# When GpSimd splits the operands of a causal attention round: two orders of one queue

## The reference

```python
x = x + 0.5 * ffn(ln(x))            # receptance and key mix with the token before
x = x + causal_attention(ln(x))     # 16 heads of 8 channels
x = x + 0.5 * ffn(ln(x))            # the same weights again
x = x + 0.5 * mixture(ln(x))        # 8 experts, the best 2 of each token
x = x + focus_attention(ln(x))      # up to 3 iterations of a second attention
x = x + 0.5 * mixture(ln(x))
```

```python
xr = mu_r * x + (1 - mu_r) * x_prev
xk = mu_k * x + (1 - mu_k) * x_prev
out = sigmoid(xr @ W_r.T) * (square(relu(xk @ W_k.T)) @ W_v.T)        # ffn

a = where(causal, q @ k.T * HD ** -0.5, -inf)                         # attention
a = clip(a, -100, 100); e = exp(a - max(a))
p = e / (sum(e) + 1e-6) + 1e-8
o = (p / sum(p)) @ v; out = o @ w_proj.T
```

## Time and profile before

| | |
|---|---|
| median of 3 runs | 1373.71 us (1372.26 to 1373.77) |
| the profiled execution's own time | 1369.53 us |
| its span, first to last instruction | 1367.8 us |
| mean granted TensorE clock | 0.966 of full speed |
| TensorE busy (share of the span) | 1217.5 us (89%) |
| VectorE busy | 920.0 us (67%) |
| ScalarE busy | 842.2 us (62%) |
| GpSimd busy | 533.9 us (39%) |
| first 50 us | setup |
| 50 to 382 us | the 16 causal rounds |
| 382 us to the end | mixture, focus attention, mixture |

### The profile page before, as it was taken

The page is one execution under the profiler, slowest core; times in us unless marked ns, Lnnn a source line. Parts: engine busy times, 40 slices in busy tenths (PEclk is TensorE's granted clock), DMA queues, the critical chain, the costliest instruction groups (busy, mean ns, idle before and its releaser), DMA issues. The chain is left out here.

```text
span 1367.8 us, 36731 instructions
## 1 busy us (share of the span) xinstructions
PE 1217.5 (89%) x12275; PEld 781.6 (57%) x12275; DVE 920.0 (67%) x2874; ACT 842.2 (62%) x1549; POOL 533.9 (39%) x817
## 2 busy tenths in 40 slices
PE   4689899898759999999889988999899997999998
PEld 3456566566537777777544433444344443767876
DVE  3578888887746874677677745666766665677444
ACT  3467777776433344443677877899787885333543
POOL 6366766766430040401344433344333331032344
PEclk9799999999959999999999999999999999999999
DMA  6323323324204022111545544445434441001332
GB/s 162 93 66 93 97 58 104 92 64 106 53 7 139 3 76 84 55 32 52 142 120 155 151 126 113 144 137 141 126 111 126 122 119 39 1 28 41 102 115 85
DMA packets 113582, 125.77 MB, mean 92 GB/s; under 512 B 14988, under 2 KB 90020, under 8 KB 113450
## 3 DMA queue, kind: packets, MB, share of 16 engines
q1 hardware_dynamic: 110378, 117.82, 30.6%
q0 software_dynamic: 3072, 6.30, 1.5%
HBM read 79.89 MB, written 44.05 MB: 91 GB/s over the span
## 5 line engine op out<-in xcount | busy, mean ns | idle before, releaser
L1469 ACT ACTIVATE e_buf<-ps_q 128x1024 f32<-128x1024 f32 x192 | 196.9, 1026 | 58.0 <-PE ps_q L2194 57.7
L2207 PE MATMUL ps_o<-e_buf,v_st 128*32 128x256 f32 x3072 | 210.7, 393 | 5.1 <-POOL v_st L1081 4.2
L1469 ACT ACTIVATE e_buf<-ps_k 128x1024 f32<-128x1024 f32 x192 | 197.0, 1026 | 7.5 <-PE ps_k L2194 7.4
L2054 PEld LDWEIGHTS ps_o<-w,e_buf 128*128 128x128 f32 x1280 | 152.2, 193 | 13.1 <-issue 12.0
L2054 PE MATMUL ps_o<-w,e_buf 128*128 128x128 f32 x1280 | 158.4, 277 | 0.0
L2622 DVE TENSOR_REDUCE mx<-ps_q 128x10 f32<-128x640 f32 x128 | 104.9, 820 | 45.0 <-PE ps_q L1752 44.1
L1290 ACT ACTIVATE e_buf<-ps_k 128x768 f32<-128x768 f32 x128 | 103.0, 805 | 46.2 <-PE ps_k L1764 45.3
L2207 PEld LDWEIGHTS ps_o<-e_buf,v_st 128*32 128x32 f32 x3072 | 81.5, 110 | 76.6 <-issue 40.3
L940 POOL TENSOR_SCALAR_AFFINE_SELECT e_buf<-e_buf 128x512 f32<-128x512 f32 x128 | 85.6, 669 | 89.8 <-ACT e_buf L1290 86.9
L1385 ACT ACTIVATE e_buf<-ps_q,b_t 128x512 f32<-128x512 f32 x80 | 54.6, 685 | 90.5 <-PE ps_q L2046 86.7
L1385 ACT ACTIVATE e_buf<-ps_k,b_t 128x512 f32<-128x512 f32 x80 | 54.0, 685 | 71.0 <-PE ps_k L2046 67.6
(11 more groups left out here) (392 smaller groups left out, 2746.5 us busy)
## 6 DMA issues: line engine op xcount, KB each, us to landing
k_st<-scr_x SPq DMA_DIRECT2D x128, 256.0 KB
q_st<-scr_q SPq DMA_DIRECT2D x256, 96.0 KB
scr_q<-parts SPq DMA_DIRECT2D x64, 192.0 KB, 2.0
scr_x<-parts SPq DMA_DIRECT2D x48, 192.0 KB, 2.0
q_st<-scr_q SPq DMA_DIRECT2D x128, 64.0 KB
slots_in<-heads_out SPq DMA_DIRECT2D x3, 1536.0 KB
slots_out<-heads_out SPq DMA_DIRECT2D x18, 256.0 KB
heads_out<-slots_in SPq DMA_DIRECT2D x15, 256.0 KB
```

Of the source, the lines that this page charges most:

```text
L1469: act.activation(e_buf[g % 2][:, hp * 2 % HG:hp * 2 % HG + 2, :], (ps_q, ps_k)[hp % 2][:, :, :], ACT.Exp).then_inc(sem("fast_exp"), 1)
L2054: last = mm(ps_o[:, e % 2, t * P:(t + 1) * P], h_sb[e % 2][:, f, t * P:(t + 1) * P], w2[:, e * NF + f, :], start=f == 0, stop=f == NF - 1)
L2207: last = mm(ps_o[at:at + VW, p, low:low + T], v_st[p][:, kt, h, :], e_buf[g % 2][:, j, kt * T:(kt + 1) * T], start=g == 0 and kt == 0, sto ...
```

## The change

Only GpSimd's program of a causal round is changed; no instruction is added to the kernel and none taken away. L916 and L920, which split the operands of a sequence, move from round n (for sequence n + 1, between masks 2 and 3) to the end of the round before, between mask 8 and the addition of the second ffn. L924 moves from behind mask 3 to the place between the mix step and mask 2. The square and the sum of the first ffn now follow mask 3 directly.

```diff
             def causal_round(n, p, half):
                 first, second, after = within(n, 0, B - 4), within(n, 2, B), within(n, 0, B - 2)
-                parts_next = within(n, 1, B - 2)
                 causal_keep(n, 0)
                 if first:
                     mix_step(mix1(n + 3), norm1(n + 3))
+                if within(n, 1, B - 2):
+                    causal_last_parts(n + 1)
                 causal_keep(n, 1)
-                if parts_next:
-                    causal_parts(n + 1)
                 causal_keep(n, 2)
-                if parts_next:
-                    causal_last_parts(n + 1)
                 if first:
                     mix_square(mix1(n + 3))
                     mix_gate(mix1(n + 3))
...
                 causal_keep(n, 7)
+                if within(n, 0, B - 3):
+                    causal_parts(n + 2)
                 if second:
                     mix_add(mix2(n - 2), n - 2)
```

## The result

The changed kernel is slower. Its median is 1382.21 us (5 runs, 1378.81 to 1385.82), before's 1373.71 us (5 runs, 1372.26 to 1374.62); the ratio is 1.0069, 95% interval 1.0045 to 1.0093. The profiled execution took 1382.21 us with a span of 1380.4 us, against 1369.53 and 1367.8.

A forecast was written before the change was run, and what follows sets the result against it. No engine is full; a cycle through the engines bounds the kernel, with VectorE not idling in its longest stretch. Rounds 2 to 12 at +0.86 us plus edges give +9.2 us, forecast 1382.9 us, range 1371 to 1391.

The forecast's parts named there:

- (b): VectorE's idle gap behind L2668, waiting for TensorE's row scores: 0.36 us a round, forecast to become 0.
- Step 1: At the round's end L916 holds up VectorE's pair L2576, so the row maxima come 0.54 us later.
- Step 2: TensorE's next row scores and VectorE's second row maxima both move by the same 0.54 us.
- Step 4: L924 blocks VectorE's L2592, then mask 2 blocks L2593, which ends 1.65 us later.
- Step 5: From L2593 to L2668 order and length stay; the square no longer makes TensorE wait.
- (a): VectorE's stretch without idling from the last row maxima to L2668's end: 12.31 us, forecast 13.96.
- Step 6: Behind the second row maxima wait, L2593 no longer meets mask 5: 2.89 us becomes 2.46; the round is +0.86 us.
- (c): VectorE's stretch from the end of its idle gap to the end of the two L2576: 2.89 us, forecast 2.46.
- (d): Stretch in which TensorE works from the transposes to the last row scores: 5.11 us, forecast unchanged.
- The number of rounds and the edges: Rounds 2 to 12 at +0.86 us each, round 1 +0.4, rounds 13 and 14 -0.36 each; +9.2 us in all.
- the gain comes through: Rival: VectorE gets the port whenever it asks, 12 rounds lose at least 0.36 us, 1369.4 us; chance 0.17.
- half the price: Rival: VectorE wins after L2592 and its pair gets ahead of L916; round about +0.3 us, 1377 us; chance 0.17.

The follow-up runs named there:

- the memset: Changed kernel with L924 behind mask 2 and, ahead of mask 2, a memset of an unread tile that only writes SBUF; rounds of 20.36 us.
- the wait for F_mix: Changed kernel in which L924, still ahead of mask 2, first waits for VectorE's L2592 and L2593; rounds of 20.81 and 20.89 us.
- the port-free versions: Changed kernel with L916 ahead of mask 8, L920 behind the addition, L924 behind mask 2, with or without mask 2 waiting for L2593; ratio 0.9906 each.

## Why the prediction was right

The forecast was 1382.9 us, the median 1382.21. The interval of the ratio puts the loss at 6 to 13 us, so the forecast's 9.2 is within it, and that the two medians meet to 0.7 us is luck. The whole is closer than its parts. Point by point:

- *What bounds the kernel*: right. Of TensorE's wait of 1.39 us only the gap (b) was the cycle's. The run without split, and the one with L924 behind the sum, show it from two sides: TensorE's wait goes and 1.39 us never come.
- *The gain of 0.36 us*: right, (b) is gone.
- *Step 1*: right in kind; the pair is 0.44 us longer, forecast 0.54.
- *Step 2*: undersized. The second row maxima come 0.80 us later in the round (135.49 - 129.96 against 136.93 - 132.20), forecast 0.54. I had let TensorE's row scores set them; it is the second pair L2575, 1.40 us, each of whose halves waits for one of GpSimd's instructions, which now follow without a gap.
- *Step 4*: right in kind, a little too large where it ends. L2592 ends 8.28 us into the round against 6.77, +1.51, forecast +1.65. L2591 starts 0.80 us later in the round, forecast 0.83, but for another reason: step 4 had it wait for the mix step, and it is the late row maxima of step 2 that it waits for. L2591 takes 1.24 us (forecast 1.3), and mask 2 got in ahead of the second one, which takes 0.85 us. The two themselves are 0.70 us longer than before. The run with L924 one place later shows that L924's place is worth 0.79 us of the round, and the memset and the wait for F_mix that it is the port.
- *Step 5 and (a)*: 13.95 us, forecast 13.96. Two misses cancel: step 4 ends 0.14 us below its +1.65, and the stretch from there to L2667, whose length step 5 left as it was, grows by 0.13 us, since the sum L884 now stands beside L2661 (0.65 us instead of 0.42).
- *Step 6*: right, (c) 2.44 (2.46), (d) 5.11 (5.11). The round is 21.43 us, forecast 21.53: +0.77 and not +0.86, of which 0.07 is that (b) falls below zero.
- *The number of rounds and the edges*: wrong in detail. Round 2, priced at +0.86, gets 0.71 us faster on the other chips, where both kernels run it at full clock: the prediction took rounds 3 and 4 for it, and missed that VectorE idles there, and that the transfer behind L924, priced at nothing, made TensorE wait 0.52 us. That is read from rows; no run changed round 2 alone. Rounds 13 and 14 were to gain 0.36 each, and round 13 loses 0.16. The sum at full clock is 7.1 us instead of 9.2.
- *The clock*: missing from the sum. In the profiled executions it took 1.3 us in each of rounds 5, 7 and 9, gave some 2 us back in rounds 1 and 2, where before had it, and may be part of the 3.6 us behind the causal stage. The median of 1382.21 contains it; whether it is also why the ratio is 1.0069 on one chip and 1.0036 on another is not shown. By the full-clock rounds alone I was 2 us too high. So the number is right partly by luck, the sign and the mechanism are not.
- *The rivals*: "the gain comes through" and "half the price" are out by L2591's 1.24 us and mask 2 ahead of L2592. A wait of TensorE for masks 1 or 2, named as what would refute me, is not the cost: all its weight loads' waits for masks at the value products make 6.3 us in rounds 3 to 15, against 5.4 before.

## What to carry to other kernels

Before a step is moved on GpSimd, write VectorE's instructions of the new place beside it and mark those with two SBUF inputs and the SBUF-to-SBUF ones in float32 (here `tensor_scalar`): in the rows of this kernel each of them ends only behind the SBUF-reading GpSimd instruction that was there first, and this kernel's cycle runs through six of them ahead of the third row maxima. A wait in the profile is worth only as much as the next engine in the cycle is ready before it; here (b), 0.36 us of 1.39. And a good place is one where GpSimd idles while VectorE reads PSUM: moved there, the same three instructions cost nothing in the steady rounds.

## What was not expected of the hardware

A second blocking instruction replaces the first one's block instead of adding to it: doubling L924 cost 0.50 us, 1.37 - 0.85 at the second VectorE instruction, and not 1.15.

TensorE's granted clock falls to the lower level in single rounds, and which ones differs between executions of the same kernel (5, 7, 9 and then 5, 11). What TensorE did before it, in round 5 of the changed kernel:

```profile
159.72 1.22 PE L1695 MATMUL ps_m<-w_t,mix 128*128 128x128 f32 x4 [0.99 <-DVE mix L2592]
```

It had idled 0.99 us and then runs L1695 at 1.22 us instead of 0.71. Round 4 has the same idle time (138.29) and no fall, so the idle alone does not decide. Over rounds 3 to 11, kernels with that wait show more falls: the change 3 and 2 of 9, the one with L924 twice 6 of 9; before 0 and 1, and L924 behind mask 2, the memset, the wait for F_mix, no split and the port-free versions none, L924 behind the sum 1. The two go together in these few executions; the cause was not isolated.
